# Three cross-attentions as one unrolled stream of units, with the next pair's preparation between them

## The reference

```python
q, k, v = split_heads(norm(x) @ wq + bq), split_heads(ctx @ wk + bk), split_heads(ctx @ wv + bv)
score = einsum('bhqd,bhkd->bhqk', q, k) * inv + mask * -1e9     # or where(mask, -1e20, score)
y = einsum('bhqk,bhkd->bqhd', softmax(score), v)
x = x + (y @ wo + bo)                                          # L1X has no output projection
```

## Time and profile before

| | us |
|---|---|
| median of 3 runs (1794.29 to 1795.9) | 1794.96 |
| profiled execution, its own time | 1792.7 |
| its span, first to last instruction | 1790.7 |
| TensorE busy in the span | 1496.2 (84%) |
| VectorE busy in the span | 1062.5 (59%) |
| ScalarE busy in the span | 728.9 (41%) |
| mean granted TensorE clock | 0.928 |

### The profile page before, as it was taken

One profiled execution on the slowest core, in us unless ns is written; L12 is line 12 of the kernel. 1 busy time (PEld: TensorE's weight loads), 2 busy tenths in 40 slices (PEclk: granted clock), 3 DMA queues, 4 the chain that ended last, 5 costly groups with the idle time before them and its releaser, 6 DMA issues.

```text
span 1790.7 us, 25936 instructions
## 1 busy us (share of the span) xinstructions
PE 1496.2 (84%) x8925; PEld 1083.2 (60%) x8925; DVE 1062.5 (59%) x2273; ACT 728.9 (41%) x1214; POOL 103.0 (6%) x129
## 2 busy tenths in 40 slices
PE   6999999777779876787779999999988888888446
PEld 5665666555544443665566778787847484847345
DVE  3434434688777655778778161616167777775434
ACT  2312121456555654545442122222228474757122
POOL 0000000000000000001000000000000000000233
PEclk9999999888889997989989999999999899989579
DMA  9340000400000000000029500000000000000077
GB/s 322 104 141 0 0 0 0 158 12 11 11 0 1 1 1 12 12 3 8 11 98 342 163 1 2 1 2 2 31 6 2 6 0 5 0 5 0 22 250 232
DMA packets 56607, 88.58 MB, mean 49 GB/s; under 512 B 10419, under 2 KB 48428, under 8 KB 56366
## 3 DMA queue, kind: packets, MB, share of 16 engines
q1 hardware_dynamic: 54142, 72.08, 12.7%
q10 hardware_dynamic: 512, 11.11, 1.8%
q0 software_dynamic: 1872, 4.27, 0.6%
HBM read 65.74 MB, written 38.35 MB: 58 GB/s over the span
## 4 chain that ended last, share of the span: by engine, by line
issue 44%; PE 33%; DVE 9%; ACT 4%; DVEq 4%; DMA 2%; POOL 1%; ACTq 1%; SPq 1%; POOLq 0%
PE bank L1757 6%; PE bank L1758 6%; PE bank L1820 3%; PE bank L1577 3%; DVE plo L823 3%; PE bank L1597 2%; PE bank L1579 2%; DMA jx<-copy_routed 2%; PE bank L1531 2%; PE bank L1689 1%; ACT hq L1324 1%; ACTq L1323 1%; ACT phi L1265 1%; PE bank L1714 1%; DVEq L1018 1%
## 5 line engine op out<-in xcount | busy, mean ns | idle before, releaser
L823 DVE TENSOR_TENSOR plo<-e,phi 120x512 f16<-120x512 f32 x256 | 185.5, 741 | 85.7 <-ACT phi L1265 80.0
L1597 PE MATMUL bank<-Q,Kpad 128*120 128x256 f16 x1024 | 209.3, 287 | 8.6 <-ACT MBT L1257 8.6
L1271 ACT ACTIVATE e<-bank 120x512 f32<-120x512 f32 x256 | 152.7, 597 | 67.6 <-PE bank L1602 37.4
L778 DVE TENSOR_REDUCE MB<-bank 128x4 bf16<-128x480 f32 x256 | 149.9, 650 | 17.9 <-PE bank L1579 11.8
L1265 ACT ACTIVATE phi<-e 120x512 f16<-120x512 f32 x256 | 158.1, 623 | 0.0
L1577 PE MATMUL bank<-Kpad,Q 128*128 128x480 f16 x256 | 108.5, 424 | 56.3 <-issue 32.5
L1601 PE MATMUL bank<-MBT,selm 128*120 128x256 bf16 x512 | 143.8, 281 | 0.0
L1602 PE MATMUL bank<-MBT,sels 128*120 128x256 bf16 x512 | 143.8, 281 | 0.0
L1620 PE MATMUL bank<-V,phi 120*128 120x34 f16 (+1 forms) x1024 | 85.4, 176 | 56.1 <-DVE plo L823 55.0
L1597 PEld LDWEIGHTS bank<-Q,Kpad 128*120 128x120 f16 x1024 | 117.3, 138 | 10.7 <-ACT MBT L1257 10.7
L1495 PE MATMUL bank<-xT,winT 128*127 128x512 f32 (+1 forms) x256 | 114.8, 594 | 4.7 <-ACTq L1185 4.7
(11 more groups left out here) (270 smaller groups left out, 2907.8 us busy)
## 6 DMA issues: line engine op xcount, KB each, us to landing
copy_routed<-zeros SPq DMA_DIRECT2D x1, 17028.0 KB
jw<-copy_experts SPq DMA_DIRECT2D x23, 641.0 KB, 4.8
h1w<-copy_h1T SPq DMA_DIRECT2D x1, 4096.0 KB, 18.9
h2w<-copy_h2T SPq DMA_DIRECT2D x1, 4096.0 KB, 14.1
ctxp<-in_ctxT SPq DMA_DIRECT2D x13, 240.0 KB, 2.6
jx<-copy_routed SPq DMA_DIRECT2D x23, 132.0 KB, 4.9
m<-in_mask SPq DMA_DIRECT2D x9, 240.0 KB, 2.7
copy_experts<-in_w1e SPq DMA_DIRECT2D x2, 1024.0 KB
```

The source lines that it names most:

```text
L778: dve.tensor_reduce(MB[:, t, h0 // 8, SK + h0 % 8:SK + h0 % 8 + 4], bank[2 + n % 4][:, 0:4 * SK].rearrange("p (h k) -> p h k", h=4), AX.X, ...
L823: dve.tensor_tensor(plo[:, u % 3, :], e32[:, u % 3, :], phi[:, u % 3, :], ALU.subtract).then_inc(s.lo, 1)
L1271: act.activation(e32[:, u % 3, :], bank[2 + u % 4][0:SK, :], ACT.Exp).then_inc(s.exp, 1)
L1597: pe.matmul(ps, Kpad[:, v, r, g, b * SK:b * SK + SK], Q2[:, g, qs], start=(v == 0), stop=False)
```

## The change

Each of the three attentions becomes one unrolled list of steps per engine, from `-n` (n = number of units) to the last unit of pair 3 and a few steps more. At step `16 i + u` (32 in L3X) an engine does its part of unit `u` of pair `i`, and then whatever of pair `i+1`, `i+2` or `i-1` is listed for `u`. `Q2`, `Kpad`, `MBT` and `V2` exist twice. The maxima tiles have two banks (5 and 6) in place of four, except for pair 0, the scores three in place of four (2 to 4), and bank 7 serves transposed maxima, values, turned output and projection in turn. Sums are folded out of PSUM eight times a pair (half as many columns each). The value rows of L1X move from ScalarE to VectorE. The table of positions, and the loop of each engine:

```diff
+        self.quarter = heads // 4
+        self.first, self.last = (3, 11) if heads == 16 else (3, 27)
+        self.turned = (5, 6) if heads == 16 else (6, 8)
+        self.projected = (7, 8) if heads == 16 else (10, 12)
+        self.flipped = (9, 10, 11, 13) if heads == 16 else (14, 18, 23, 29)
+        self.keyed, self.valued, self.columned = heads - 3, heads - 2, heads - 1
+        self.lows = (4, 5, 6, 7) if heads == 16 else (4, 6, 8, 10, 12, 14, 16, 18)
+        self.split, self.stated, self.normed = (5, 10, 12) if heads == 16 else (5, 20, 23)
+        self.checked = 12
+    def tiles(self, u):
+        return min(max(-(-self.approx * (u - self.first + 1) // (self.last - self.first + 1)), 0), self.approx)
...
+            mask(0)
+            value_rows(0)
+            for step in range(-n, PAIRS * n + L.projected[1] + 1):
+                i, u = step // n, step % n
+                ahead, after, before = 0 <= i + 1 < PAIRS, 0 <= i + 2 < PAIRS, 0 <= i - 1 < PAIRS
+                if 0 <= step - 2 < PAIRS * n:
+                    low_part(step - 2)
+                sg, rest = (step - 3) // (n // 8) - 1, (step - 3) % (n // 8)
+                if rest == 0 and 0 <= sg < 8 * PAIRS:
+                    consume(sg)
+                sg, rest = (step - 4) // (n // 8) - 1, (step - 4) % (n // 8)
+                if rest == 0 and sg % 2 and 0 <= sg < 8 * PAIRS:
+                    normalise(sg)
+                if ahead and u == 0:
+                    split_keys(i + 1)
+                if ahead and u in (1, 2):
+                    if u == 1:
+                        dve.drain()
+                    padded_keys(i + 1, u - 1)
+                    low_queries(i + 1, u - 1)
+                if ahead:
+                    for m in range(L.tiles(u - 1), L.tiles(u)):
+                        maxima(i + 1, m)
+                if ahead and u == L.split:
+                    split_values(i + 1)
+                if L is not L1X and before and u in L.projected:
+                    projected(i - 1, L.projected.index(u))
+                if 1 <= i + 2 <= PAIRS and u == L.stated:
+                    norm_stats(ph, i + 1)
+                if 1 <= i + 2 <= PAIRS and u == L.normed:
+                    norm_rows(ph, i + 1)
+                if L is L2X and 0 <= i < PAIRS and u == L.checked:
...
+                if 1 <= i + 2 < PAIRS and u == L.valued:
+                    mask(i + 2)
+                if 1 <= i + 2 < PAIRS and u == L.columned:
+                    value_rows(i + 2)
...
+            for step in range(-n, PAIRS * n + L.turned[1] + 1):
+                i, u = step // n, step % n
+                ahead, before = 0 <= i + 1 < PAIRS, 0 <= i - 1 < PAIRS
+                if 0 <= step - 1 < PAIRS * n:
+                    exponential(step - 1)
+                if 0 <= step - 2 < PAIRS * n:
+                    high_part(step - 2)
+                if ahead and u in (1, 2):
+                    high_queries(i + 1, u - 1)
+                if ahead and u in L.lows:
+                    low_keys(i + 1, L.lows.index(u))
+                if ahead and u in L.flipped:
+                    maxima_rows(i + 1, L.flipped.index(u))
+                if L is not L1X and before and u in L.turned:
+                    output_columns(i - 1, L.turned.index(u))
+                if 1 <= i + 2 < PAIRS and u == L.valued:
+                    keys(i + 2)
+                if 1 <= i + 2 <= PAIRS and u == L.columned:
+                    evacuate_xT(4 * ph + i + 3, 5)
...
+            def approximate(j, m):
+                t, q = m // L.quarter, m % L.quarter
...
+                deep = 4 if j == 0 else 2
+                if m >= deep:
+                    pe.wait_ge(s.red, L.a0 + j * L.approx + m - deep + 1)
...
+            def scores(g):
+                i, u = g // n, g % n
+                if u == 0:
+                    pe.wait_ge(s.mbt, TT * (L.c0 + i) + TT)
+                    pe.wait_ge(s.klow, L.c0 + i + 1)
+                if g >= 3:
+                    pe.wait_ge(s.exp, L.u0 + g - 2)
...
+            for step in range(-n, PAIRS * n + L.projected[1] + 1):
+                i, u = step // n, step % n
+                ahead, before = 0 <= i + 1 < PAIRS, 0 <= i - 1 < PAIRS
+                if 0 <= step < PAIRS * n:
+                    scores(step)
+                if 0 <= step - 3 < PAIRS * n:
+                    values(step - 3)
+                if ahead and u in (0, 1):
+                    queries(i + 1, u)
+                if ahead:
+                    for m in range(L.tiles(u - 1), L.tiles(u)):
+                        approximate(i + 1, m)
+                if L is not L1X and before and u in L.turned:
+                    turn_output(i - 1, L.turned.index(u))
+                if L is not L1X and before and u in L.projected:
+                    project(i - 1, L.projected.index(u))
+                if ahead and u in L.flipped:
+                    transpose_maxima(i + 1, L.flipped.index(u))
+                if 1 <= i + 2 < PAIRS and u == L.keyed:
+                    keys(i + 2)
+                if 1 <= i + 2 < PAIRS and u == L.valued:
+                    values_in(i + 2)
+                if 1 <= i + 2 <= PAIRS and u == L.columned:
+                    if i + 2 < PAIRS:
+                        pe.wait_ge(s.k32, L.c0 + i + 3)
+                    transpose_rows(4 * ph + i + 3, 5)
```

More of the change, by code:

```diff
@@ L343, in build @@
         if L is not L1X:
[L344 removed]
+            s.oT, s.oTs, s.out, s.half, s.bo = (sem(L.name + "_" + n) for n in ("oT", "oTs", "out", "half", "bo"))
         X[L.name] = s
@@ L733, in prepare @@
                         else:
[L734 to L743, removed]
+                            last = dve.tensor_scalar(MB[:, :, h, 0:SK], m32[:], NEG_ADD, None, ALU.mult)
@@ L754, in attention, with padded_keys @@
[L754 to L762, removed]
+            def padded_keys(j, part):
+                if j >= 2 and part == 0:
+                    dve.wait_ge(s.sc, L.u0 + (j - 1) * n)
+                for r in range(part * HG // 2, (part + 1) * HG // 2):
+                    last = dve.tensor_scalar(K[j % 2][:, 0, r, :, :], khi[:], rm[:, r:r + 1], None, ALU.mult)
+                if part == 1:
+                    dve.drain().then_inc(s.kpad, 1)
@@ L783, in attention, with maxima @@
[L783 to L787, removed]
+            def maxima(j, m):
+                t, h0 = m // hq, 4 * (m % hq)
+                dve.wait_ge(s.ap, L.a0 + j * L.approx + m + 1)
+                b = bank[(5, 6, 2, 3)[m % 4] if j == 0 else 5 + m % 2]
+                dve.tensor_reduce(MB[:, t, h0 // 8, SK + h0 % 8:SK + h0 % 8 + 4],
+                                  b[:, 0:4 * SK].rearrange("p (h k) -> p h k", h=4), AX.X, ALU.max).then_inc(s.red, 1)
@@ L1233, in keys_and_values @@
[L1233 to L1243 removed]
+                        last = act.activation(k32[:, g, :], ps, ACT.Identity, bias=bias2[:, c:c + 1], scale=L.scale)
@@ new lines, in values @@
+            def values(g):
+                i, u = g // n, g % n
+                b, sg = u // (n // 2), g // (n // 8)
+                if sg >= 2 and g % (n // 8) == 0:
+                    pe.wait_ge(s.pvc, 8 * L.c0 + sg - 1)
+                if u == 0:
+                    pe.wait_ge(s.v2, L.c0 + i + 1)
+                pe.wait_ge(s.lo, L.u0 + g + 1)
+                for q in range(2):
+                    h = 2 * (u % (n // 2)) + q
+                    rhs = v2(L, b, i)[:, h, :, :].rearrange("p v d -> p (v d)")
+                    for t in range(2):
+                        c0 = (t * L.quarter + h % L.quarter) * 2 * (dh + 1)
+                        ps = bank[sg % 2][:, c0:c0 + 2 * (dh + 1)]
+                        cols = slice(q * S + t * 128, q * S + t * 128 + 128)
+                        pe.matmul(ps, phi[:, g % 3, cols], rhs, start=True, stop=False)
+                        last = pe.matmul(ps, plo[:, g % 3, cols], rhs, start=False, stop=True)
+                last.then_inc(s.pv, 1)
@@ new lines, in turn_output, with project @@
+            def turn_output(i, k):
+                if k == 0:
+                    pe.wait_ge(s.o, L.c0 + i + 1)
+                else:
+                    pe.wait_ge(s.oTs, 2 * (L.c0 + i) + 1)
+                for t in range(TT):
+                    last = pe.transpose(bank[7][:, tok(t)], o[:, t, k * 128:k * 128 + 128], ident[:])
+                last.then_inc(s.oT, 1)
+            def project(i, h):
+                if h == 0:
+                    pe.wait_ge(s.oTs, 2 * (L.c0 + i) + 2)
+                else:
+                    pe.wait_ge(s.half, L.c0 + i + 1)
+                for t in range(2):
+                    for k in range(K2):
+                        last = pe.matmul(bank[7][:, t * D:t * D + D], oT[:, k, tok(2 * h + t)], w[3][:, k, :],
+                                         start=(k == 0), stop=(k == K2 - 1))
+                last.then_inc(s.out, 1)
```

467 lines of the change are left out of this document (211 added, 256 removed).

## The result

| | before | after |
|---|---|---|
| median, us | 1795.4 (4 runs) | 1766.9 (4 runs, 1765.3 to 1769.4) |
| ratio, 95% interval | 1 | 0.9842 (0.9825 to 0.9859) |
| profiled execution, us | 1792.7 | 1767.7 |
| its span, us | 1790.7 | 1765.6 |
| VectorE busy, us | 1062.5 | 1067.9 |

What follows compares the result with a forecast made beforehand. VectorE was taken to bound L1X and L2X, level with TensorE in L3X. Ends of 33 us less shorter periods gave -4, +6 and -19, together -17: 1775.7 us profiled, 1778 beside the median, range 1738 to 1818.

Steps and rivals of the forecast that it cites:

- Floors and steady periods: Overlapped pairs: work and gaps of the busiest engine, 41.8, 49.4, 67.0 us; with waits, periods of 45, 56.4, 75.
- Seam: Where one pair passes to the next: VectorE waits about 2 us in L1X, 5.5 in L2X, 5 in L3X.
- Middle: Mid-pair, ScalarE's waits for transposed maxima and turned output cost 1 us a pair, 1.5 in L2X, 3 in L3X.
- waits of over 1 us: Sign of being wrong: ScalarE's waits for transposed maxima reappear as such `plo` waits four times a pair.
- VectorE busy above 85% of a stream: Sign expected in the profile after: VectorE's busy share within a pair of the stream above 85%.
- L1X 6 - 3 x (48.2 - 45): L1X's sum: 6 us of ends less three equal periods' gains, -4; likewise L2X +6 and L3X -19.
- The ends: Start and finish of each attention: 6 us added in L1X, 15 in L2X, 12 in L3X, 33 together.
- the table load: ScalarE's table loads lie beside TensorE's queries and cost 0.
- Dense streams: Rival, chance 0.26: pair boundary and middle cost next to nothing, periods 43, 51 and 70, total 1741 us.
- ScalarE's waits paid in full or by half: Rival, chance 0.22: six steps a pair where ScalarE waits for TensorE cost time; 1817 us by half, 1855 in full.
- The queues: Rival, chance 0.05: engines wait out each other's extras, periods stay, 33 us are added, 1828.
- the clock's rival: Rival, chance 0.03: TensorE at half clock half the time; pairs 48, 62, 102 us in L1X, L2X, L3X; 1885.

Runs made afterwards that it cites:

- e_dve: Changed kernel with VectorE taking the next pair's row statistics three times instead of once: 1806.1 us, ratio 1.0053 to the kernel before.
- e_evac: Changed kernel with ScalarE's copies of the next pair's transposed rows one step later, behind step 0's exponential: 1748.2 us, ratio 0.9735 to the kernel before.
- e_low15: Changed kernel with `low_bits` of L2X's pairs moved from step 12 to step 15, behind the value rows: 1756.7 us, ratio 0.9792 to the kernel before.
- e_pe: Changed kernel with TensorE making the first product of each of the maxima's tiles twice: 1785.9 us, ratio 0.9936 to the kernel before.
- e_act2: Changed kernel with ScalarE making each copy of the transposed maxima twice: 1773.5 us, ratio 0.9873 to the kernel before.
- e_table: Changed kernel with a one-element exponential heading each attention's ScalarE list, to load its table early: 1766.3 us, ratio 0.9846 to the kernel before.
- e_start: Changed kernel with pair 1's preparation moved from each attention's front to behind its first units: 1760.9 us, ratio 0.9807 to the kernel before.
- e_best: Changed kernel with `xT` copies behind step 0's exponential, last pair's `low_bits` behind the last normalise, exponential table loaded early: 1740.2 us, ratio 0.9685 to the kernel before.

## Why the prediction was right

It forecast 1778 within 1738 to 1818, faster; 1766.9 was measured. The view that VectorE's work plus a chain at the seam sets the periods holds, and e_dve, e_evac and e_low15 show it; e_pe adds a share of TensorE's in L2X and L3X, and e_act2 ScalarE's in L3X. That the total came out so near is luck: the periods gave 30 us more than forecast, and the ends took 20 us more.

**Floors and steady periods: right.** The steady (middle) periods are 44.0, 54.5 and 77.5 us against 45, 56.4 and 75; three times their sum is 528 against 529. Of L1X's 44.0, 39.35 are busy and 2.7 waits, so 1.95 are gaps, against 1.9 taken; the floor is 41.3 against 41.8. In L3X 77.5 less waits of 11.3 leaves 66.2 against a floor of 67, and the waits are 3.3 us more than the 8 taken. Two of the halved reductions took 0.51 us [0.52 taken].

**Seam: right in place and cause.** The longest single wait for `phi` is 2.5, 4.7 and 2.8 us against 2, 5.5 and 5, behind the transposes, and in L2X at the clock of 0.50 that was foreseen. In L3X the forecast's 5 counts steps 29 to 31, and a second wait stands there, behind ScalarE's copies of the keys (1.83 us, the last row below): 4.6 together. What was not seen is that the chain could be cut: the exponential needs no part of it.

**Middle: right for L1X and L2X, low for L3X**, where the other waits for `phi` are 3.7 us and those for TensorE's tiles 2.1, against 3. VectorE in that stream:

```profile
1464.31 0.69 DVE L832 TENSOR_TENSOR plo<-e,phi 120x512 f16<-120x512 f32 x1 [1.20 <-ACT phi L1325]
...
1471.39 0.69 DVE L832 TENSOR_TENSOR plo<-e,phi 120x512 f16<-120x512 f32 x1 [1.10 <-ACT phi L1325]
...
1498.54 0.69 DVE L832 TENSOR_TENSOR plo<-e,phi 120x512 f16<-120x512 f32 x1 [1.83 <-ACT phi L1325]
```

The first two stand behind ScalarE's copies of transposed maxima (at 1462.67 and 1469.76). They are waits of over 1 us, which the prediction named as a sign of being wrong if they came four times a pair: they came twice, and in L3X alone. Of its other signs, VectorE busy above 85% of a stream was met only in L1X (89%, against 84 and 82).

**The step that failed is "L1X 6 - 3 x (48.2 - 45)" and its two like it:** three equal periods per attention. The first stream has nothing left over from a pair before and is shorter than the middle one by 5.3, 6.5 and 7.7 us; VectorE is busy 7.4, 7.8 and 6.5 us less in it. The third prepares no keys, values or mask and has no bias sum on GpSimd beside it: shorter by 2.4 in L2X, 7.5 in L3X, with VectorE busy 2.1 and 3.2 us less (0.6 longer in L1X, which this does not explain). That is 29 us, nearly the whole difference between the 50 us of periods forecast and the 80 measured.

**The ends were mis-sized too: 33 forecast, 53 measured.** The first unit is late by 9.4, 11.4 and 14.0 instead of 6, 8.4 and 10.2. I had added the work of pair 1 and not the waits between the engines that do it in turn: between 346.8 and 354.8 ScalarE does 3.9 us of work and waits 4.0. Of that work 1.28 us is the table load, taken at 0 because it had lain beside TensorE's queries; now it stands just ahead of the exponential. e_table shows no gain from moving it. The last pair of L2X cost 14.4 instead of 6.5: `low_bits` bare as foreseen, but TensorE behind it at half clock, and again in the projection, which waits for copies and residuals in turn. e_start joins the two misses: what is brought ahead of the first unit comes off the first stream, so a forecast that counts the one in full must shorten the other.

**The rivals.** Dense streams (1741) has periods of 43, 51 and 70, which are near those of e_evac's middle streams, 42.0, 51.7 and 73.9: that is about what mending the seam gives. That e_best ran at 1740 is no proof of it, since its periods sum to 481 us against the rival's 492 and its ends cost some 40 where the rival has 33. ScalarE's waits paid in full or by half did not come in L1X and L2X; e_act2 shows the mechanism in L3X. The queues did not serialise. In the sum of the clock's rival 39.4 x 1.5 is 59 us for L2X, not 62, so it should have read some 1876; it changes nothing else. TensorE kept its clock in the streams, 0.87 to 0.98. L3X's third stream, 32 tiles on two banks, ran at 0.98, and behind the 7 us for which TensorE stood at `low_bits` the clock was 0.50. The Trainium skill (TensorE: Matmul & The Clock Gate, A second HAM failure mode: psum-queue depth-cycling) would have it swing where matmuls cycle through banks with short idles between; by that rule L3X's third stream, whose 32 tiles go through two banks, should have shown it, and at 0.98 it does not.

## What to carry to other kernels

When a loop is unrolled into one stream, price its first, middle and last passes apart: the first has no leftovers and pays its preparation ahead, the last has nothing to hide it. In the stream, look for the engine that stands at a wait with ready work queued behind it. Here two lines that let the exponential pass the copies of `xT` gave 20 us, some 70% of what the whole change gave. Slack in one engine's list is filled by moving work it has to do anyway: `low_bits` cost 4 us less per pair three steps later.

## What the runs showed of the hardware that was not expected

The bias sum on GpSimd slows some of VectorE's instructions beside it and not others. The `low_bits` of L2X's middle stream began with it (GpSimd 805.41 to 808.25), and VectorE's rows are:

```profile
806.11 1.22 DVE L627 TENSOR_REDUCE lowmax<-low 128x1 f32<-128x1024 int32 x1
807.25 2.08 DVE L624 TENSOR_SCALAR low<-h1w 128x2048 int32<-128x2048 int32 x1
```

The reduction takes 1.22 us as always; the bitwise one, which goes over 2048 elements where the reduction has 1024, takes 2.08, and 1.22 in the third stream with GpSimd idle. In e_low15 the bias sum (797.52 to 800.32) falls on a `plo` instead, which takes 2.25 us for its usual 0.69:

```profile
798.61 2.25 DVE L832 TENSOR_TENSOR plo<-e,phi 120x512 f16<-120x512 f32 x1
```

The Trainium skill (GPSIMD Engine Reference, Specifications) says that the two engines share their ways into SBUF, with contention for VectorE's instructions with two SBUF inputs or in a two-port mode; these rows agree, and show what it costs, 0.9 and 1.6 us. In both cases that is a little less than the time for which the instruction lay beside the sum (1.0 and 1.7 us), as if it had stood until the sum was over. A `plo` that began 0.11 us ahead of the sum (797.41) took its usual 0.69.
